# Three PSUM banks in turn, DVE work in half-chunk order, and the low part of x1 on GpSimd

## The chip, the cores and the metric

The kernel runs on one core of one Trainium2 chip. The metric is device time in microseconds (us), the median of the runs shown. Engines are named as in the profile: PE (TensorE), DVE (VectorE), ACT (ScalarE), POOL (GpSimd), SP (the queue that issues the DMAs). Each engine works through its own list of instructions in order, and semaphores order the engines against each other.

## The reference

```python
# layer 0, x: (4, 256, 64, 64)
k = conv(x, w1, 7x7, dilation 2, padding 6) + b1        # 256 -> 128 channels
k = conv(k, w2, 1x1) + b2                               # 128 -> 49 channels
attn = softmax(k, axis=1)                               # 49 weights at each pixel
x1 = einsum('bkchw,bkhw->bchw', shifts(x, 7x7, dilation 2), attn)
# layer 1: a bottleneck with batch norms over (0, 2, 3)
h = relu(bn(conv(x1, v1, 1x1)));  h = relu(bn(conv(h, v2, 3x3)));  h = bn(conv(h, v3, 1x1))
out = relu(h + x1)
```

## The kernel before

Because of the dilation by 2, each image splits into four independent images of 32x32 pixels ("images" from here on, 16 in all, `STEPS`). w1 and w2 are folded into one set of filters of 50 columns. Every fp32 operand of a product is split into a high part (rounded to fp32r) and a low part (the rest), and a product takes three matmuls (`mm3`). So each operand passes through an ACT copy (`..._hi`) and a subtraction (`..._lo`), on DVE or POOL.

**Preparation** (0 to 84 us). PE computes 14 groups of folded filters (L805, 14 matmuls in the profile for each) into the two banks `psX` in turn, ACT copies them (`wf`, `w_hi`), DVE forms sums of them (`filters`, L1036) and some low parts, POOL the other low parts (`filter_lo`). Between them DVE and POOL prepare the first signals of the convolution.

**The main loop** runs over 20 halves (`half(q)` of each engine), two for each pair of images. A Winograd-like convolution of a pair is 14 chunks (`ORDER`: points TWO, ONE, MINUS, HALF1, MHALF, ZERO, INF, for two channel blocks); an even half has the first 7, an odd half the last 7. Each chunk needs a signal: a sum of columns of `xbuf` (`whole`, L1063 on DVE or L546 on POOL), its high part (`sig_hi`, ACT) and its low part (`sig_lo`, POOL L551), in a ring of five. For point TWO DVE also rewrites the input buffer (`ab_of`: L1083 and L1089), and POOL then rewrites it once more (`c_of`, L558, 2304 columns in one instruction). `combine` (DVE, L1128 to L1147) forms the logits of ten output columns from the banks 0 to 2 of the points. In the next even half the softmax follows (`softmax_top`, `exponentials`, `softmax_end`), and its weights go out to DRAM and come back as bands (`scatter`, `load_raw`).

Three halves behind the convolution the same loop works on an image: PE transposes 8 band tiles (`band_T`, L848, all through the bank `psB`) and 4 pieces of x (`x_T`, L858, through `psXT`). ACT and DVE split them; ten `unit`s (L782 to L784) multiply them into `psX`, five for each half of the image's rows. `x_out` then copies `psX` to `x1_hi` and `x1` (ACT) and forms `x1_lo` (DVE, reading `psX`); `proj` (L888, through `psU`) multiplies x1 with v1; `yhalf` (ACT) and `y_out` (DVE, L1203 and L1205) finish it. "image" is the one at work, "tail" the one before it, whose second row half is finished in this half. PE walks through 15 parts in a half (two for each chunk), the others through 7 steps c.

After the loop come the batch norms, the 3x3 and the last 1x1 convolution (835 to 1031 us), which the change does not touch.

Of the kernel before, what the change touches and what calls it, by code (L numbers as in the profile page):

```python
# [9 lines left out]
ALU = mybir.AluOpType  # L10
# [104 lines left out]
(C_ONE, C_BIAS, C_SUM, C_DIFF, C_TWO), C_HALF, C_MHALF, C_ZERO, C_INF, COMBOS = range(5), 8, 12, 16, 17, 18  # L115


def build(nc, x, w1, b1, w2, b2, v1, g1, c1, v2, g2, c2, v3, g3, c3, out):
# [6 lines left out]
    with top:  # L125
# [9 lines left out]
        psXT, psB, psU = ps[:, 5, :], ps[:, 6, :], ps[:, 7, :]  # L135

# [17 lines left out]
        bias = sb(l0r, "bias", [P, KP])  # L154
# [77 lines left out]
        norm_done, probs_done = sem("norm_done"), sem("probs_done")  # L232
# [77 lines left out]
        def wait_slot(eng, g, t):  # L310

            if t >= 4:
                eng.wait_ge(unit_done, len(UNITS) * g + last_unit(t - 4) + 1)
            elif g:
                eng.wait_ge(unit_done, len(UNITS) * (g - 1) + last_unit(t + 4) + 1)

# [30 lines left out]
        def _(sp):  # L347
# [99 lines left out]
            def half(q):  # L447
                conv, first, image, tail, coming, soft = schedule(q)
                if tail is not None:
                    store_x1(tail, 1)  # L450
                if soft is not None:
                    spill(soft, 0)
# [64 lines left out]
        def _(pool):  # L517
            for t in (ident[:, :], gavg[:, :], up[:, :, :], dn[:, :, :], w2T[:, KK:KP], b2row[:, KK:KP]):
                pool.memset(t, 0.0).then_inc(consts, 1)
            for t in (ones[:, :], inside[:, :, :]):  # L520
                pool.memset(t, 1.0).then_inc(consts, 1)
            for c0, c1 in ((0, 2 * PAD), (2 * PAD + W, XC)):
                pool.memset(xbuf[:, :, 0:SH * XC].rearrange("p i (r c) -> p i r c", c=XC)[:, :, :, c0:c1], 0.0).then_inc(consts, 1)
            pool.memset(xbuf[:, :, SH * XC:XLEN], 0.0).then_inc(consts, 1)
            pool.wait_ge(consts, 11)
# [51 lines left out]

            def slot(k):

                if 0 <= k + RING - 1 < NCHUNK:  # L580
                    signal(k + RING - 1)
                if 0 <= k + RING - 2 < NCHUNK:
                    sig_lo(k + RING - 2)
                for i in range(2 * PAIRS):
                    if k == chunk_at(i // 2, TWO, i % 2) - RING + 3:
# [3 lines left out]

            for i in range(5):  # L590
                filter_lo(i)
            for k in range(1 - RING, 0):
                slot(k)
# [22 lines left out]
        def _(act):  # L616
# [6 lines left out]
            act.wait_ge(consts, 11)  # L623
# [12 lines left out]
            for i in range(CB * K):  # L636
                cb, v = divmod(i, K)
                act.wait_ge(weff_done, i + 1)
                if v in DIRECT:
                    copy(w_hi[:, cb, DIRECT[v], :], psX[i % 2][:, 0:NF]).then_inc(whi_done, 1)  # L640
                if cb:
                    act.wait_ge(wmade, MADE[3] if v <= 3 else MADE[6])
                copy(wf[:, v, :], psX[i % 2][:, 0:NF]).then_inc(wf_done, 1)
# [3 lines left out]
                if (cb, v) == (0, 5):  # L647
                    for k in range(RING - 2):
                        sig_hi(k)
# [19 lines left out]
            def xT(g, pt):  # L669
                act.wait_ge(xt_done, 4 * g + pt + 1)  # L670
                wait_slot(act, g, 2 * pt + 1)
                copy(xT_hi[:, 2 * pt % 4:2 * pt % 4 + 2, :], psXT.rearrange("p (t c) -> p t c", c=C)).then_inc(xT_hi_done, 1)

            def bandhi(g, t):
# [3 lines left out]
                copy(by_fours(band_hi[:, t % 4, band_rows(t), :]), window_of(psB[:, lo:hi])).then_inc(band_hi_done, 1)  # L678

            def yhalf(g, h):  # L680
# [3 lines left out]
                copy(y1[:, h, :], psU[MID1:P, :]).then_inc(yhalf_done, 1)  # L684
# [4 lines left out]

            def half(q):  # L690
                conv, first, image, tail, coming, soft = schedule(q)
                for c in range(SLOTS):
                    if image is not None:
                        if c in (0, 1, 2):
                            bandhi(image, c)
                    if c == 0 and tail is not None:
                        x_out(tail, 1)
                    if c == 0 and image is not None:
                        xT(image, 0)
                    if c == 2 and image is not None:  # L700
                        xT(image, 1)
                    if c == 3 and image is not None:
                        bandhi(image, 3)
                    if conv is not None and first + c + RING - 2 < NCHUNK:
                        sig_hi(first + c + RING - 2)
                    if c == 1 and tail is not None:
# [648 lines left out]
```

## Time and profile before

| what | value |
|---|---|
| median of 3 runs | 1032.48 us (1031.37 to 1032.67) |
| profiled execution, its own time | 1033.16 us |
| its span | 1031.4 us |
| mean granted TensorE clock | 0.940 of full speed |

The span runs from the first to the last instruction of the profiled execution; 1.8 us lie around it. Rows of a timeline give the start, the duration, the engine, the line, the operation with its tiles, and in brackets how long the engine sat idle before and what ended that.

### The profile page before, as it was taken

Reading aid. Unit: us, or ns where it says so; the run is one execution under the profiler, and the core shown is the slowest. Engines: PE = TensorE matmul, PEld = TensorE weight load, DVE = VectorE, ACT = ScalarE, POOL = GpSimd, SP = SyncE. Lnnn points to the kernel's source line nnn. Section 1 sums busy time; section 2 is a strip of 40 time slices with the busy share of each in tenths; the row PEclk is TensorE's granted clock in tenths of the full one; section 3 lists DMA queues with packets and bytes.
Section 4 is the critical chain, followed back from the end, with each engine's and each line's share of the span. In section 5 each row is a group of like instructions: output and inputs, shape, how many; then the busy total and the mean of one; then the engine's idle time right before and its main releaser. Section 6 shows DMA issues by size and latency. Waiting matters only on the chain.

```text
span 1031.4 us, 13805 instructions
## 1 busy us (share of the span) xinstructions
PE 870.8 (84%) x5084; PEld 815.1 (79%) x5084; DVE 670.4 (65%) x913; ACT 378.2 (37%) x647; POOL 321.5 (31%) x257
## 2 busy tenths in 40 slices
PE   5548969898998998999899899899667649969992
PEld 5548969898998998999899799899656537758882
DVE  1765677567778678676667767855544455139994
ACT  1222211243333433344344243333333466133267
POOL 2536455263255245227224524422200000004000
PEclk9999989999999999999899999999867869989997
DMA  9600224966775794885577576464687977000099
GB/s 287 211 0 1 42 53 104 204 176 149 166 194 133 172 202 114 207 178 163 156 173 180 146 174 151 124 188 109 177 206 194 209 269 296 1 1 1 26 388 401
DMA packets 261851, 163.11 MB, mean 158 GB/s; under 512 B 203817, under 2 KB 244762, under 8 KB 259226
## 3 DMA queue, kind: packets, MB, share of 16 engines
q1 hardware_dynamic: 261786, 162.24, 58.7%
q8 instruction: 41, 0.67, 0.3%
q14 instruction: 24, 0.20, 0.1%
HBM read 103.41 MB, written 53.97 MB: 153 GB/s over the span
## 4 chain that ended last, share of the span: by engine, by line
PE 49%; DVE 26%; DMA 8%; issue 7%; ACT 5%; POOL 2%; SPq 2%; DVEq 0%; ACTq 0%; POOLq 0%
PE ps L782 13%; PE ps L783 13%; PE ps L784 13%; DVE logit L1156 4%; DVE logit L1147 4%; DVE whole L1063 3%; PE ps L848 3%; DVE xbuf L1083 3%; DMA dn<-logit 3%; PE ps L888 3%; PE ps L805 2%; ACT y L774 2%; PE ps L858 2%; DMA out<-y 2%; DVE wsum L1036 2%
## 5 line engine op out<-in xcount | busy, mean ns | idle before, releaser
L782 PE MATMUL ps<-w_hi,ring 128*128 128x350 f32 x832 | 282.5, 340 | 12.1 <-DVE logit L1147 11.4
L784 PE MATMUL ps<-w_hi,ring 128*128 128x350 f32 x832 | 273.9, 329 | 0.0
L783 PE MATMUL ps<-w_lo,ring 128*128 128x350 f32 x832 | 273.5, 329 | 0.0
L551 POOL TENSOR_TENSOR ring<-whole,ring 128x576 fp32r<-128x576 f32 x112 | 168.2, 1503 | 263.5 <-ACT ring L618 263.5
L782 PEld LDWEIGHTS ps<-w_hi,ring 128*128 128x128 f32 x832 | 162.2, 195 | 13.4 <-issue 12.8
L783 PEld LDWEIGHTS ps<-w_lo,ring 128*128 128x128 f32 x832 | 161.8, 194 | 0.5
L784 PEld LDWEIGHTS ps<-w_hi,ring 128*128 128x128 f32 x832 | 160.9, 193 | 0.0
L618 ACT ACTIVATE ring<-whole 128x576 fp32r<-128x576 f32 x112 | 86.4, 775 | 142.3 <-DVE whole L1063 100.2
L618 ACT ACTIVATE band_hi<-ps 128x320 fp32r<-128x320 f32 (+1 forms) x128 | 53.6, 419 | 190.9 <-PE ps L848 190.7
L782 PE MATMUL ps<-band_hi,xT_hi 128*128 128x224 f32 (+2 forms) x320 | 99.2, 310 | 17.0 <-DVE x_lo L1000 10.0
L1000 DVE TENSOR_TENSOR band_lo<-ps,band_hi 128x320 fp32r<-128x320 f32 (+1 forms) x128 | 58.8, 459 | 72.5 <-ACT band_hi L618 72.4
L848 PE MATMUL ps<-ident,raw 128*128 128x128 f32 x352 | 64.8, 290 | 46.3 <-DVE band_lo L1000 42.5
L782 PE MATMUL ps<-h_hi,v_hi 128*128 128x512 f32 x224 | 90.9, 406 | 12.3 <-DVE h_lo L1000 12.3
L784 PE MATMUL ps<-band_hi,xT_lo 128*128 128x224 f32 (+2 forms) x320 | 95.2, 298 | 0.0
L783 PE MATMUL ps<-band_lo,xT_hi 128*128 128x224 f32 (+2 forms) x320 | 95.1, 297 | 0.0
L783 PE MATMUL ps<-h_lo,v_hi 128*128 128x512 f32 x224 | 90.4, 404 | 0.0
L784 PE MATMUL ps<-h_hi,v_lo 128*128 128x512 f32 x224 | 90.0, 402 | 0.0
L848 PEld LDWEIGHTS ps<-ident,raw 128*128 128x128 f32 x352 | 43.9, 148 | 56.5 <-issue 51.1
L1063 DVE SCALAR_TENSOR_TENSOR whole<-xbuf 128x576 f32<-128x576 f32 x80 | 74.5, 934 | 15.0 <-POOL ring L551 15.0
L782 PEld LDWEIGHTS ps<-band_hi,xT_hi 128*128 128x128 f32 x320 | 63.7, 199 | 20.6 <-DVE x_lo L1000 10.7
L612 POOL TENSOR_TENSOR h_lo<-y,h_hi 128x1024 fp32r<-128x1024 f32 x6 | 14.2, 2414 | 190.8 <-ACT h_hi L618 190.8
L1000 DVE TENSOR_TENSOR xT_lo<-ps,xT_hi 128x512 fp32r<-128x512 f32 x64 | 43.8, 685 | 42.3 <-ACT xT_hi L618 42.3
(127 smaller groups left out, 1435.2 us busy)
## 6 DMA issues: line engine op xcount, KB each, us to landing
xq<-in_x SPq DMA_DIRECT2D x128, 256.0 KB, 4.0
raw<-bands SPq DMA_DIRECT2D x32, 768.0 KB, 5.5
xbuf<-in_x SPq DMA_DIRECT2D x16, 1024.0 KB, 8.5
x_dram<-x SPq DMA_DIRECT2D x32, 512.0 KB, 2.8
x1in<-x_dram SPq DMA_DIRECT2D x8, 2048.0 KB, 17.0
out<-y SPq DMA_DIRECT2D x16, 1024.0 KB, 4.5
bands<-wide SPq DMA_DIRECT2D x32, 398.0 KB, 5.5
w1raw<-in_L_conv_w SPq DMA_DIRECT2D x2, 3136.0 KB, 12.6
```

Source lines behind the costliest of these rows:

```text
L551: pool.tensor_tensor(split(k, 1), positions(whole[:, k % TBUFS, :], 0, 2), split(k, 0).bitcast(F32), ALU.subtract).then_inc(sig_lo_done, 1)
L618: return act.activation(dst, src, ACT.Copy)
L782: pe.matmul(dst, l_hi, r_hi_, start=first, stop=False, **kw)
L783: pe.matmul(dst, l_hi, r_lo_, start=False, stop=False, **kw)
L784: return pe.matmul(dst, l_lo, r_hi_, start=False, stop=last, **kw)
L848: mm = pe.transpose(psB[:, i * P:(i + 1) * P], src, ident[:, :])
L888: mm = pe.matmul(psU, v1pack[:, cb, :], r[:, cb, :], start=(cb == 0 and j == 0), stop=(cb == CB - 1 and j == 1))
L1000: return dve.tensor_tensor(dst, a, b, ALU.subtract)
L1063: dve.scalar_tensor_tensor(out=dst, in0=a, scalar=factor, in1=b, op0=ALU.mult, op1=ALU.add).then_inc(done, 1)
L1083: dve.scalar_tensor_tensor(out=flat[:, 0:n], in0=flat[:, 0:n], scalar=-2.0, in1=flat[:, 2:n + 2], op0=ALU.mult, op1=ALU.add).then_inc(a_do ...
L1147: dve.scalar_tensor_tensor(out=dst, in0=m, scalar=factor, in1=src, op0=ALU.mult, op1=ALU.add).then_inc(comb_done, 1)
L1156: dve.scalar_tensor_tensor(out=part, in0=t[:, :, :], scalar=edge[:, i:i + 1], in1=part, op0=ALU.mult, op1=ALU.add).then_inc(add_done, 1)
```

## The change

Eight edits, all in the preparation and the main loop:

1. **Banks.** The filter groups use four banks (`psW`) instead of two. In the loop `band_T`, `x_T` and `proj` take the banks 5, 6 and 7 in one fixed rotation (`turns`): each waits for whoever used its bank three turns ago.
2. **Low part of x1.** `x_lo` on POOL reads `x1` and `x1_hi` from SBUF; `psX` is free as soon as ACT has copied it. In the three last halves, with no convolution, DVE does it.
3. **Order.** DVE and ACT go through 14 half-chunk parts. `proj(tail, 1)` moves from part 3 to 5 on PE, `proj(image, 0)` from part 13 to 14; `y_out(image, 0)` to the next half, and `y_out(tail, 1)` behind `softmax_end`.
4. **Combine.** 15 operations instead of 18 for a pair: the bias is added in the first one; ACT forms the product of HALF1 (`half_product`); the odd half has two operations on PSUM and four on SBUF alone, all behind the last MHALF chunk, where there were four behind HALF1 and four behind MHALF.
5. **c_of** in four pieces of 576 columns, each waiting for the one before.
6. **Softmax end**: one large product and a small one (112 columns) instead of two large ones.
7. **First signals** are made by DVE and POOL right after the first filter group.
8. **SP** spills logits ahead of `store_x1(tail, 1)`.

```diff
+        psW = [ps[:, 3, :], ps[:, 4, :], ps[:, 7, :], ps[:, 6, :]]
...
+            for kind, of, i in (("band", image, 0), ("x", image, 0), ("band", image, 1), ("band", image, 2),
+                                ("proj", tail, 1), ("x", image, 1), ("band", image, 3), ("band", image, 4),
+                                ("x", image, 2), ("band", image, 5), ("band", image, 6), ("x", image, 3),
+                                ("band", image, 7), ("proj", image, 0)):
+                if of is not None:
+                    turns.append((kind, of, i))
...
+        def take_bank(eng, kind, g, i):
+            n = turn_of[kind, g, i]
+            if n >= 3:
+                before, gb, ib = turns[n - 3]
+                if before == "band":
+                    eng.wait_ge(band_lo_done, NT * gb + ib + 1)
+                elif before == "x":
+                    eng.wait_ge(xT_lo_done, 4 * gb + ib + 1)
+                else:
+                    eng.wait_ge(y1_done, 2 * gb + ib + 1)
...
             def c_of(i):
                 pool.wait_ge(b_done, i + 1)
-                n = 2 * (SH * XC // 2)
-                pool.tensor_tensor(xflat(i)[:, 0:n], xflat(i)[:, 4:n + 4], xflat(i)[:, 0:n], ALU.subtract).then_inc(c_done, 1)
+                n = SH * XC // 4
+                for j in range(4):
+                    if j:
+                        pool.wait_ge(c_done, 4 * i + j)
+                    a, b = (xflat(i)[:, o + n * j:o + n * (j + 1)] for o in (0, 4))
+                    pool.tensor_tensor(a, b, a, ALU.subtract).then_inc(c_done, 1)
...
             def slot(k):
-                if 0 <= k + RING - 1 < NCHUNK:
+                q, c = divmod(k, SLOTS)
+                conv, first, image, tail, coming, soft = schedule(q)
+                if c == 1 and tail is not None:
+                    x_lo(tail, 1)
+                if c == 6 and image is not None:
+                    x_lo(image, 0)
+                if k + RING - 1 < NCHUNK:
                     signal(k + RING - 1)
...
                     if k == chunk_at(i // 2, TWO, i % 2) - RING + 3:
                         c_of(i)
```

ACT, `half`:

```diff
+                        if part == 10:
+                            bandhi(image, 6)
+                        if part == 11:
+                            x_out(image, 0)
...
+                    if part % 2 and conv is not None and first + part // 2 + RING - 2 < NCHUNK:
+                        sig_hi(first + part // 2 + RING - 2)
```

DVE, `half`:

```diff
+                        todo = ({10: (C_ONE,), 12: range(C_SUM, C_EVEN)} if q % 2 == 0 else
+                                {6: range(C_EVEN, C_ZERO), 12: (C_ZERO,)})
...
+                    if part == 7 and soft is not None:
+                        softmax_end(soft)
+                    if part == 7 and tail is not None:
                         y_out(tail, 1)
...
+                    if part % 2 and conv is not None:
+                        signal_slot(first + part // 2)
```

**POOL at the end of an odd half with an image.** The names: `whole<-pairs` is a signal, `ring<-whole,ring` a `sig_lo`, `xbuf<-xbuf` is `c_of`, `x_lo` the new low part of x1. Before:

```order
L546 TENSOR_TENSOR whole<-pairs 128x576 [waits sig_lo_done,b_done]
L551 TENSOR_TENSOR ring<-whole,ring 128x576 [waits sig_hi_done]
L546 TENSOR_TENSOR whole<-pairs 128x576 [waits sig_lo_done,b_done]
L551 TENSOR_TENSOR ring<-whole,ring 128x576 [waits sig_hi_done]
L558 TENSOR_TENSOR xbuf<-xbuf 128x2304 [waits b_done]
L551 TENSOR_TENSOR ring<-whole,ring 128x576 [waits sig_hi_done]
```

And now:

```order
L581 TENSOR_TENSOR ring<-whole,ring 128x576 [waits sig_hi_done]
L576 TENSOR_TENSOR whole<-pairs 128x576 [waits sig_lo_done,b_done]
L581 TENSOR_TENSOR ring<-whole,ring 128x576 [waits sig_hi_done]
L592 TENSOR_TENSOR xbuf<-xbuf 128x576 [waits b_done]
L592 TENSOR_TENSOR xbuf<-xbuf 128x576 [waits c_done] x3
L615 TENSOR_TENSOR x_lo<-x,x_hi 128x512 [waits x1_done] x2
```

The two `x_lo` stand behind the four pieces of `c_of`, and these behind a `sig_lo` that waits for ACT.

**DVE in an odd half, from the combine behind MHALF to the input rewrite.** `logit`, `mo` and `me` belong to combine, `whole`, `xbuf` and `pairs` to the signal of the next point TWO. Before:

```order
L1147 SCALAR_TENSOR_TENSOR logit<-ps,logit 128x500 [waits comb_done,chunk_done] x4
L1000 TENSOR_TENSOR band_lo<-ps,band_hi 128x320 [waits unit_done,band_hi_done] x2
L1063 SCALAR_TENSOR_TENSOR whole<-xbuf 128x576 [waits pads_done,x_loaded2,sig_lo_done]
L1063 SCALAR_TENSOR_TENSOR whole<-xbuf,whole 128x576 [waits sig_step]
L1083 SCALAR_TENSOR_TENSOR xbuf<-xbuf 128x2308 [waits sig_dve]
L1089 SCALAR_TENSOR_TENSOR pairs<-xbuf 128x1152 [waits sig_pool,a_done]
```

And now:

```order
L1209 SCALAR_TENSOR_TENSOR mo<-ps,me 128x500 [waits chunk_done,half_done,comb_done]
L1209 SCALAR_TENSOR_TENSOR me<-ps,me 128x500 [waits chunk_done,comb_done]
L1209 SCALAR_TENSOR_TENSOR logit<-mo,logit 128x500 [waits comb_done]
L1209 SCALAR_TENSOR_TENSOR logit<-me,logit 128x500 [waits comb_done]
...
L1066 TENSOR_TENSOR xT_lo<-ps,xT_hi 128x512 [waits unit_done,xT_hi_done]
L1066 TENSOR_TENSOR band_lo<-ps,band_hi 128x320 [waits unit_done,band_hi_done]
L1268 TENSOR_TENSOR y<-ps,y 64x512 [waits yhalf_done]
L1270 BN_STATS stats<-y 64x6 [waits y1_done]
L1130 SCALAR_TENSOR_TENSOR whole<-xbuf 128x576 [waits pads_done,x_loaded2,sig_lo_done]
```

Six operations (the two on `logit` come twice) now stand where four stood, and one `xT_lo` and `y_out(tail, 1)` have come in ahead of the signal.

**PE at the fifth band tile (t = 4).** `ident,raw` is `band_T`, `w_hi,ring` the convolution, `band_hi,xT_hi` a unit. Before:

```order
L784 MATMUL ps<-w_hi,ring 128x350
L848 MATMUL ps<-ident,raw 128x128 [waits band_lo_done,raw_loaded1,raw_loaded0]
L848 MATMUL ps<-ident,raw 128x128 x2
L782 MATMUL ps<-band_hi,xT_hi 128x320 [waits xT_lo_done,band_lo_done]
L783 MATMUL ps<-band_lo,xT_hi 128x320
```

And now:

```order
L842 MATMUL ps<-w_hi,ring 128x350
L909 MATMUL ps<-ident,raw 128x128 [waits y1_done,raw_loaded1,raw_loaded0]
L909 MATMUL ps<-ident,raw 128x128 x2
L840 MATMUL ps<-w_hi,ring 128x350
L841 MATMUL ps<-w_lo,ring 128x350
```

The tile waited for the `band_lo` before it; it now waits for `y_out(tail, 1)`, whose bank it takes, and its unit comes half a chunk later.

## Rows read from the trace of the kernel before

**Rows 1.** The page: span and busy time of the engines.

```profile
span 1031.4 us, 13805 instructions
...
PE 870.8 (84%) x5084; PEld 815.1 (79%) x5084; DVE 670.4 (65%) x913; ACT 378.2 (37%) x647; POOL 321.5 (31%) x257
```

**Rows 2.** Windows: preparation, loop with images, last halves (stretch, length, busy).

```profile
0.00:84.00 84.00, 45.71 (x204) 44.70 (x204) 44.80 (x63) 18.59 (x40) 33.97 (x41) 1.00 0.52 153
...
191.00:721.00 530.00, 496.48 (x3269) 483.94 (x3267) 377.67 (x508) 199.41 (x362) 210.49 (x156) 0.98 0.67 164
721.00:835.00 114.00, 74.36 (x419) 66.28 (x417) 51.85 (x90) 42.22 (x89) 5.33 (x12) 0.78 0.76 190
```

**Rows 3.** Timeline of PE in the preparation: filter groups.

```profile
12.91 18.66 PE L805 MATMUL ps<-w2T,w1raw 128*128 128x50 f32 x84 [2.48 <-DMA w1raw<-in_L_conv_w]
...
64.66 12.48 PE L805 MATMUL ps<-w2T,w1raw 128*128 128x50 f32 x56 [14.78 <-DVE w_lo L1000]
```

**Rows 4.** Timeline of PE: an odd half (268.85 on), the even half behind it.

```profile
268.85 0.38 PE L848 MATMUL ps<-ident,raw 128*128 128x128 f32 x2
287.64 0.52 PE L848 MATMUL ps<-ident,raw 128*128 128x128 f32 x3 [0.48 <-DVE band_lo L1000]
295.36 0.28 PE L782 MATMUL ps<-band_hi,xT_hi 128*128 128x96 f32 x1 [0.97 <-DVE xT_lo L1000]
302.53 0.48 PE L888 MATMUL ps<-x_hi,v1pack 128*128 128x512 f32 x1
307.61 0.38 PE L848 MATMUL ps<-ident,raw 128*128 128x128 f32 x2
326.43 0.52 PE L848 MATMUL ps<-ident,raw 128*128 128x128 f32 x3 [3.53 <-DVE band_lo L1000]
353.85 0.38 PE L848 MATMUL ps<-ident,raw 128*128 128x128 f32 x2
```

**Rows 5.** Timeline of DVE in the same odd half.

```profile
284.07 3.03 DVE L1147 SCALAR_TENSOR_TENSOR logit<-ps,logit 128x500 f32<-128x500 f32 x4
289.07 0.76 DVE L1063 SCALAR_TENSOR_TENSOR whole<-xbuf 128x576 f32<-128x576 f32 x1
290.66 2.56 DVE L1083 SCALAR_TENSOR_TENSOR xbuf<-xbuf 128x2308 f32<-128x2308 f32 x1
293.25 1.36 DVE L1089 SCALAR_TENSOR_TENSOR pairs<-xbuf 128x1152 f32<-128x1152 f32 x1
300.46 0.68 DVE L1147 SCALAR_TENSOR_TENSOR logit<-ps,logit 128x500 f32<-128x500 f32 x1 [0.62 <-PE ps L784]
305.09 0.69 DVE L1205 BATCH_NORM_STATS2 stats<-y 64x6 f32<-64x512 f32 x1
```

**Rows 6.** Timeline of ACT there: the copies of x1, and a sig_hi.

```profile
297.90 1.11 ACT L618 ACTIVATE x<-ps 128x512 f32<-128x512 f32 x2
298.85 0.82 ACT L618 ACTIVATE ring<-whole 128x576 fp32r<-128x576 f32 x1
```

**Rows 7.** Timeline of POOL: sig_lo, c_of in both halves.

```profile
283.49 1.93 POOL L551 TENSOR_TENSOR ring<-whole,ring 128x576 fp32r<-128x576 f32 x1 [6.63 <-ACT ring L618]
...
298.46 1.43 POOL L551 TENSOR_TENSOR ring<-whole,ring 128x576 fp32r<-128x576 f32 x1
299.86 4.03 POOL L558 TENSOR_TENSOR xbuf<-xbuf 128x2304 f32<-128x2304 f32 x1
...
316.45 4.58 POOL L558 TENSOR_TENSOR xbuf<-xbuf 128x2304 f32<-128x2304 f32 x1
```

**Rows 8.** Timeline of DVE in the even half: the top of the softmax.

```profile
315.95 1.19 DVE L1156 SCALAR_TENSOR_TENSOR logit<-up,edge,logit 128x600 f32<-128x600 f32 x1 [1.65 <-DMA dn<-logit]
317.18 4.50 DVE L1156 SCALAR_TENSOR_TENSOR logit<-dn,edge,logit 128x600 f32<-128x600 f32 x1
```

**Rows 9.** Groups by line: POOL subtractions with an fp32r result.

```profile
L612 POOL TENSOR_TENSOR h_lo<-y,h_hi 128x1024 fp32r<-128x1024 f32 x6 | 14.2, 2414 | 190.8 <-ACT h_hi L618 190.8
```

**Rows 10.** Timeline of PE at the start of the second pair.

```profile
153.53 0.63 PE L782 MATMUL ps<-w_hi,ring 128*128 128x350 f32 x1 [9.59 <-DVE logit L1147]
```

More of the change, by code:

```diff
@@ L588, in slot @@
                         pads(i)
+            signal(1)
+            sig_lo(0)
+            signal(2)
+            sig_lo(1)
+            sig_lo(2)
             for i in range(5):
                 filter_lo(i)
-            for k in range(1 - RING, 0):
-                slot(k)
+            c_of(0)
             for i in range(5, CB * len(WHOLES)):
@@ L688, in exponentials, with half_product @@
                 act.activation(probs[:, :, :, :], probs[:, :, :, :], ACT.Exp).then_inc(exp_done, 1)
+            def half_product(s):
+                act.wait_ge(chunk_done, chunk_at(s, HALF1, CB - 1) + 1)
+                act.wait_ge(comb_done, comb(s, C_EVEN - 1))
+                act.activation(me[:, :], ps[:, BANKS[HALF1], 0:BANK], ACT.Copy, scale=16 / 9).then_inc(half_done, 1)
             def half(q):
                 conv, first, image, tail, coming, soft = schedule(q)
-                for c in range(SLOTS):
-                    if image is not None:
[L694 to L706, printed above, removed]
@@ new lines, in half @@
+                for part in range(2 * SLOTS):
+                    if part == 0 and tail is not None:
+                        x_out(tail, 1)
+                    if part == 4 and q % 2 == 1 and conv is not None:
+                        half_product(conv)
+                    if image is not None:
+                        if part in (0, 2, 4):
+                            bandhi(image, part // 2)
+                        if part in (1, 5, 8):
+                            xT(image, part // 3)
+                        if part == 6:
+                            bandhi(image, 3)
+                        if part == 7:
+                            bandhi(image, 4)
+                        if part == 9:
+                            bandhi(image, 5)
+                        if part == 10:
+                            bandhi(image, 6)
+                        if part == 11:
+                            x_out(image, 0)
+                    if part == 6 and tail is not None:
@@ L1240, in half @@
-                    if c == 6 and image is not None:
-                        xT(image, 3)
-                        bandlo(image, 7)
-                        y_out(image, 0)
-                    if conv is not None:
-                        signal_slot(first + c)
+                    if part == 2 and conv is None and tail is not None:
+                        x_lo(tail, 1)
+                    if part == 4 and soft is not None:
+                        softmax_top(soft)
+                    if image is not None:
+                        if part in (1, 3, 5):
+                            bandlo(image, part // 2)
+                        if part in (2, 6, 9):
+                            xT(image, (2, 6, 9).index(part))
+                        if part in (7, 8):
+                            bandlo(image, part - 4)
+                        if part in (10, 11):
+                            bandlo(image, part - 5)
```

238 lines of the change are left out of this document (118 added, 120 removed).

## The prediction

> **What bounds the kernel now.** I read the page first [rows 1]: PE is busy for 870.8 of 1031.4 us, DVE for 670.4, POOL for 321.5. So the question is where PE waits. The windows [rows 2] split it: in the preparation PE is busy for 45.7 of 84.0 us, in the 530 us of the loop with images for 496.5, in the last halves for 74.4 of 114. The timeline of PE shows what ends the waits. In the preparation it is DVE: one filter group waits 14.78 us for a `w_lo` that stands behind filter sums and the input rewrite [rows 3]. In the loop a pair takes 85.0 us (268.85 to 353.85), an odd half 38.8 and an even half 46.2 [rows 4]. The odd half has two small waits (0.48 and 0.97); the even half has one of 3.53 us at a band tile. That tile waits for a `band_lo` behind the top of the softmax, whose second operation took 4.50 us because POOL was in `c_of` from 316.45 on for 4.58 us [rows 8, 7].
>
> That row is worth a closer look. The first softmax operation came at 315.95, took 1.19 us and ended at 317.14; `c_of` was issued at 316.45 and ended at 321.03; the second operation then ended at 321.68. So whichever of the two engines waits gets the next turn, for a whole instruction. POOL waits likewise: a `sig_lo` of 1.43 us took 1.93 beside a `whole` on DVE [rows 7]. DVE's combine of 0.68 us at 300.46, which reads one operand from PSUM, lost nothing beside the `c_of` of 299.86 [rows 5, 7]. So two SBUF operands are what matters. The Trainium skill (SBUF — State Buffer, "SBUF: two separate sides") calls the shared port pair an exclusive lock, held for the whole instruction, and names DVE operations with two SBUF inputs; by this rule, the trace agrees. By a rule of shared bandwidth the third term below would be near zero.
>
> **The change, part by part.** The sum is made against the profiled execution's 1033.2 us, 0.7 above the median.
>
> *Preparation: -20 us.* A filter group takes 3.1 us (four in 12.48) and the first starts at 12.91 [rows 3]. With four banks the first eleven run on to about 47. DVE's work is still in series: sums of one block, their second part, the rewrite for the second input (1.5, 2.56 and 1.36 us, as in the loop [rows 5]); but the first rewrite now fills time in which DVE waited for filter copies. I put the `w_lo` that releases the twelfth group at 54.5. Three groups follow, and the convolution starts near 64 in place of 84.0. Bounds: -12, if DVE and the earlier `c_of` block each other more, and -24.
>
> *Combine and the fifth band tile, odd half: +3.6 us.* Before, four operations in 3.03 us (0.77 each) began at 284.07, and the tile was released at 287.64 [rows 5, 4]. Now six operations stand there (+1.55), then an `xT_lo`, `band_lo`, and `y_out`, 0.7 us each by the nearest row (0.69 at 305.09), and PE waits for the last: about 290.4 for work ready at 287.1. Behind it DVE's signal starts at 291 instead of 289.07, and a `sig_lo` of 1.4 us, which ACT now releases just then, gets in between its two operations. The rewrite (2.56 and 1.36) ends 3.3 us later, the `xT_lo` behind it too, and the unit that started at 295.36 now starts at 299.0. That PE's waits take this form is why the rotation gains little here: the bank that the tile takes is that of the slowest user.
>
> *proj(image, 0) in an odd half with c_of: +9.4 us.* Follow the queues from that unit, at 299.0. ACT copies x1 (four copies, two in 1.11 us [rows 6]), done at 302.5, and only then makes `sig_hi` (0.8), which stood ahead of the copies before. POOL's `sig_lo` ends at 304.7. Now comes `c_of`. A piece costs about 1.15 us: 4.03 / 4 = 1.0 is the lower bound [rows 7], the fixed part of an instruction adds to it. Then the two `x_lo`: half of 2.41 us for 1024 columns, 1.2 to 1.27 each [rows 9]. PE meanwhile needs 7.2 us from the unit to proj as before (295.36 to 302.53), and 1.8 more, since 12 of the 34 matmuls of the next 5.08 us now stand ahead of proj [rows 4]: it is there at 307.9. POOL alone would be done at 312.2. But DVE's two signals, 2.56 and 1.36 (5.4 us in all) are released at 305.2 by the last ZERO chunk, and turn by turn with the pieces they go in ahead of `x_lo`: it ends at 317.2, and proj waits 9.4 us. Bounds: 4.3 (no DVE operation gets in) and 10.5.
>
> *Clock: +1.6 us in each of these.* After the idle 9.59 us the first matmul took 0.63 us, twice a usual one [rows 10], and the last halves, which are full of waits, have a granted clock of 0.78, the loop 0.98 [rows 2]. I take 1.6 us, as if some 3 us of work behind the wait ran at the lower of the clock's two levels (1.2 in place of 2.4 GHz). Bounds 0 and 2.
>
> *Even half: -1.5 us, six times.* The 3.53 us go, and about 1.5 behind them (the loop's granted clock of 0.98 is 1.7 us in a pair of 85 [rows 2]), since the softmax now starts well before PE needs it. In their place the fifth tile waits for `y_out(tail, 1)` behind `band_hi`, `yhalf`, the exponentials and `softmax_end`: 2.4 us, some lock turns, and some clock. Bounds: -3 and +1.
>
> *The rest.* The half with q = 15 has no `c_of`: +3, the tile alone. The first two pairs: 0 (a shorter combine, but the pieces and the rewrite again share turns; -3 to +2). The last halves: -7 (the spill no longer waits for `store_x1`, units wait for ACT's copies alone); they idle 40 us [rows 2], bounds -15 and 0. DVE loses 64 `x_lo`, 24 combine operations and 8 large products: nothing, except where said, as DVE is idle a third of the time [rows 1].
>
> Sum: six odd halves 6 x 14.6 = 87.6, less 2.6 for the first, which has no tail (85); even halves -9; preparation -20; q = 15 +3; last halves -7; +52. So 1033.2 + 52 = 1085, less 0.7 for the median: **1084 us**. Its own range is 1066 to 1098.
>
> **The rivals.**
> - *POOL keeps its turn*: `c_of` and `x_lo` run through, and DVE follows. proj waits 4.3 instead of 9.4 us: 6 x 5.1 = 31 less, 1054 us. Against it stands the 1.19 us operation of [rows 8], which got in between two POOL instructions. Chance 0.16.
> - *The combine does not delay the unit*: the tile's wait is absorbed as the second one of 0.97 us partly is. 6 x 3.6 = 22 less, 1062 us. Chance 0.12.
> - *Faster*: the low part is ready in time, because POOL gets to `c_of` earlier than I think (it would have to start 9 us earlier relative to proj, or the queue order lets ACT release `sig_lo` before the copies). Then six halves cost 3.6 at most, or nothing, and the preparation and the last halves remain: 1033 - 20 - 7 - 9 + 3 + (0 to 20), 1000 to 1020 us. It decides at a cost of (20 + 9 + 7 - 3) / 6 = 5.5 us for an odd half; I have 14.6, and 9.5 at the lower bound of the lock. For it: DVE loses 60 us of work, and the waits of [rows 4] for `band_lo` do go. Chance 0.22.
> - *The preparation does not gain*: the twelfth group is released as late as before. Then 1104. Chance 0.04.
>
> The Trainium skill (GPSIMD Engine Reference, "Performance versus the Vector engine") has GpSimd about two times slower than DVE for such a subtraction. That alone would cost nothing here, as POOL is idle two thirds of the time; it is the place in POOL's queue that costs.
>
> **How the numbers follow.** My forecast has 0.44; rivals 0.16, 0.12, 0.22, 0.04; 0.02 for no change. A difference under 0.2% (2 us) is about what a measurement cannot tell from none. Range 1008 to 1096: it leaves out the lower half of the faster case and the preparation rival. Faster 0.22, same 0.02, slower 0.76.
>
> **What would show it.** Right: convolution starts near 64 us; in each odd half with `c_of` PE waits 8 to 10 us at proj for `x_lo` on POOL, and 2 to 4 us at the fifth band tile for `y`; DVE's `whole`, `xbuf` and `pairs` alternate with four POOL pieces; a pair takes about 98 us. Wrong: proj without a wait, or a pair under 88 us; then the order of release on POOL is not what I followed.

## The result: slower, 1082.3 us

The changed kernel takes 1082.3 us (median of 4 runs, 1082.0 to 1083.2) beside 1032.5 us for the kernel before on the same chip (4 runs): 1.0486 times the time, 95% interval 1.0472 to 1.0500. The profiled execution took 1083.2 us. Its page answers to [rows 1]:

```profile
span 1081.4 us, 13756 instructions
PE 893.0 (83%) x5084; PEld 837.8 (77%) x5084; DVE 634.3 (59%) x839; ACT 375.3 (35%) x655; POOL 438.8 (41%) x356
```

DVE is busy 36 us less, POOL 117 us more, and the span is 50 us longer: the engine that was relieved was not the one that set the time. What PE waited for (engine, line, what it waited for, us in total, times, longest), two rows of the view of waits:

```profile
PE ps L947 <- POOL x_lo L615: 46.0, 6, 8.2
PE ps L909 <- DVE y L1268: 43.8, 16, 4.9
```

The same waits in the timeline of PE: two filter groups (compare [rows 3]), then the fifth band tile of an even and of an odd half and `proj(image, 0)` of that odd half (compare [rows 4]).

```profile
38.36 9.42 PE L865 MATMUL ps<-w2T,w1raw 128*128 128x50 f32 x42 [0.68 <-DVE w_lo L1066]
55.62 0.65 PE L865 MATMUL ps<-w2T,w1raw 128*128 128x50 f32 x2 [7.85 <-DVE w_lo L1066]
64.82 0.64 PE L840 MATMUL ps<-w_hi,ring 128*128 128x350 f32 x1
235.98 0.52 PE L909 MATMUL ps<-ident,raw 128*128 128x128 f32 x3 [2.47 <-DVE y L1268]
281.32 0.52 PE L909 MATMUL ps<-ident,raw 128*128 128x128 f32 x3 [2.98 <-DVE y L1268]
306.75 0.79 PE L947 MATMUL ps<-x_hi,v1pack 128*128 128x512 f32 x1 [8.18 <-POOL x_lo L615]
```

The convolution starts at 64.8 us instead of 84.0. The fifth tile waits for `y`, and `proj`, which had no wait before, waits 8.18 us. Why it does is read from POOL and DVE in the same odd half (POOL's rows first, then DVE's, then the last two copies of x1 on ACT; compare [rows 5, 6, 7]):

```profile
293.96 1.42 POOL L581 TENSOR_TENSOR ring<-whole,ring 128x576 fp32r<-128x576 f32 x1 [1.63 <-ACT ring L668]
295.33 7.81 POOL L592 TENSOR_TENSOR xbuf<-xbuf 128x576 f32<-128x576 f32 x4
303.11 3.59 POOL L615 TENSOR_TENSOR x_lo<-x,x_hi 128x512 fp32r<-128x512 f32 x2
...
295.83 1.27 DVE L1130 SCALAR_TENSOR_TENSOR whole<-xbuf 128x576 f32<-128x576 f32 x1
297.13 1.59 DVE L1130 SCALAR_TENSOR_TENSOR whole<-xbuf,whole 128x576 f32<-128x576 f32 x1
298.75 3.39 DVE L1150 SCALAR_TENSOR_TENSOR xbuf<-xbuf 128x2308 f32<-128x2308 f32 x1
302.18 2.18 DVE L1156 SCALAR_TENSOR_TENSOR pairs<-xbuf 128x1152 f32<-128x1152 f32 x1
...
292.12 1.10 ACT L668 ACTIVATE x<-ps 128x512 f32<-128x512 f32 x2
```

x1 was copied at 293.2 (last ACT copy), PE was ready for proj at 298.58, `x_lo` ended at 306.70. Four pieces of `c_of` took 7.81 us of POOL, and the view of these four by tile shows why (minimum, median and maximum of a piece, in ns):

```profile
L592 POOL TENSOR_TENSOR xbuf<-xbuf x4: 1148/1542/3347, 295.3 to 299.8; 128x576 f32<-128x576 f32 x4
```

An undisturbed piece is 1.15 us. The last one came at 299.8, while DVE was in `xbuf`, and took 3.35 us, so it waited 2.2 us. The `xbuf` operation had waited in its turn for the piece ahead: it took 3.39 us, where 2.56 are usual [rows 5]. The Trainium skill (SBUF — State Buffer, "SBUF: two separate sides") has the shared port pair as an exclusive lock rather than shared bandwidth; the row agrees.

Behind the wait the granted clock is at its lower level (windows: stretch, length, busy time and count of PE, PEld, DVE, ACT, POOL, then the granted clock):

```profile
306.70:308.90 2.20, 2.15 (x6) 1.76 (x7) 0.00 (x0) 0.04 (x1) 2.06 (x3) 0.50 0.47 130
308.90:313.00 4.10, 4.10 (x21) 4.10 (x20) 1.37 (x2) 0.56 (x2) 0.46 (x1) 0.56 0.03 8
313.00:320.00 7.00, 7.00 (x48) 6.99 (x47) 2.74 (x4) 4.70 (x9) 3.04 (x3) 1.00 0.61 149
```

0.50 is 1.2 of 2.4 GHz. The four matmuls of proj took 2.08 us and the 18 of the units behind it 4.34; in the even half ahead, without a wait, they took 1.09 and 2.60. So 8.2 us of wait cost another 2.7 us.

Where the 50 us arise is read from the starts of `proj(image, 0)` in both timelines, a mark that every half has:

| stretch (us) | before | after | difference | forecast |
|---|---|---|---|---|
| start to proj of the first odd half with an image | 217.5 | 210.2 | -7.3 | -8 (-20 preparation, 0 first pairs, +12 that half) |
| from there five pairs, to proj of q = 13 | 425.8 | 479.9 | +54.1 | +65.5 |
| one more pair, to q = 15 (no c_of) | 84.5 | 86.7 | +2.2 | +1.5 |
| to proj of the last image's second half | 101.6 | 102.4 | +0.8 | -7 |
| the rest | 202.0 | 202.2 | +0.2 | 0 |

### The profile page after: what moved, and what is told of

It is laid out like the page before. It is cut to its first block, busy times and chain, and to the rows that moved or that the text cites. A ratio compares the mean times of both kernels' runs of the same rounds, so it can differ in the third digit from the quotient of the medians.

```text
span 1081.4 us, 13756 instructions
## 1 busy us (share of the span) xinstructions
PE 893.0 (83%) x5084; PEld 837.8 (77%) x5084; DVE 634.3 (59%) x839; ACT 375.3 (35%) x655; POOL 438.8 (41%) x356
## 4 chain that ended last, share of the span: by engine, by line
PE 54%; DVE 21%; POOL 9%; ACT 6%; DMA 4%; issue 4%; SPq 1%; ACTq 0%; DVEq 0%; POOLq 0%
PE ps L840 14%; PE ps L841 14%; PE ps L842 14%; POOL xbuf L592 4%; DVE stats L1377 4%; PE ps L947 4%; PE ps L909 3%; DVE x1in L1389 3%; PE ps L918 2%; POOL x_lo L615 2%; PE ps L865 2%; DVE logit L1209 2%; POOL ring L581 2%; ACT y L832 2%; DVE whole L1130 1%
## 5 line engine op out<-in xcount | busy, mean ns | idle before, releaser
L840 PE MATMUL ps<-w_hi,ring 128*128 128x350 f32 x832 | 288.3, 346 | 11.0 <-DVE logit L1209 10.0
L581 POOL TENSOR_TENSOR ring<-whole,ring 128x576 fp32r<-128x576 f32 x112 | 171.9, 1537 | 288.9 <-ACT ring L668 288.9
L842 PE MATMUL ps<-w_hi,ring 128*128 128x350 f32 x832 | 275.4, 331 | 0.0
L840 PEld LDWEIGHTS ps<-w_hi,ring 128*128 128x128 f32 x832 | 164.2, 197 | 11.8 <-issue 10.6
L841 PEld LDWEIGHTS ps<-w_lo,ring 128*128 128x128 f32 x832 | 163.6, 197 | 0.0
L842 PEld LDWEIGHTS ps<-w_hi,ring 128*128 128x128 f32 x832 | 162.7, 196 | 0.0
L909 PE MATMUL ps<-ident,raw 128*128 128x128 f32 x352 | 66.5, 296 | 52.0 <-DVE y L1268 43.8
L840 PE MATMUL ps<-band_hi,xT_hi 128*128 128x224 f32 (+2 forms) x320 | 102.5, 320 | 7.4 <-DVE xT_lo L1066 4.7
L592 POOL TENSOR_TENSOR xbuf<-xbuf 128x576 f32<-128x576 f32 x64 | 101.6, 1588 | 3.8
L841 PE MATMUL ps<-band_lo,xT_hi 128*128 128x224 f32 (+2 forms) x320 | 100.3, 313 | 0.0
L842 PE MATMUL ps<-band_hi,xT_lo 128*128 128x224 f32 (+2 forms) x320 | 99.8, 312 | 0.0
L1130 DVE SCALAR_TENSOR_TENSOR whole<-xbuf 128x576 f32<-128x576 f32 x80 | 81.1, 1018 | 20.4 <-POOL ring L581 20.3
L668 ACT ACTIVATE xT_hi<-ps 128x512 fp32r<-128x512 f32 x64 | 38.5, 602 | 150.7 <-PE ps L918 106.6
## 6 DMA issues: line engine op xcount, KB each, us to landing
x1in<-x_dram SPq DMA_DIRECT2D x8, 2048.0 KB, 17.1
```

The source lines that it names most:

```text
L581: pool.tensor_tensor(split(k, 1), positions(whole[:, k % TBUFS, :], 0, 2), split(k, 0).bitcast(F32), ALU.subtract).then_inc(sig_lo_done, 1)
L592: pool.tensor_tensor(a, b, a, ALU.subtract).then_inc(c_done, 1)
L668: return act.activation(dst, src, ACT.Copy)
L840: pe.matmul(dst, l_hi, r_hi_, start=first, stop=False, **kw)
L841: pe.matmul(dst, l_hi, r_lo_, start=False, stop=False, **kw)
L842: return pe.matmul(dst, l_lo, r_hi_, start=False, stop=last, **kw)
```

## Experiments

The kernel before was measured again on the chip of each run below, and took 1031.3 to 1032.7 us there.

**Theory.** In an odd half three results come out of their queues within a few us of each other: `y_out` behind the combine (DVE), `x_lo` behind `c_of` (POOL), and the low parts `xT_lo` and `band_lo` behind the rewrite (`xbuf`, `pairs`, DVE). The change made all three late; the one that PE meets first shows in the trace and hides the others. **Rival.** The position of `x_lo` on POOL alone is the loss, and putting it right gives it back. A second rival is that the two engines share bandwidth, so that the number of pieces and the order don't matter.

### before_prep: the preparation alone

The kernel before, with four banks for the filter groups, the first signals behind the first filter copy, and POOL's order there; its loop is untouched.

```diff
-                if (cb, v) == (0, 4):
+                if (cb, v) == (0, 0):
                     for k in range(1 - RING, -1):
                         signal_slot(k)
...
-                    mm = pe.matmul(psX[i % 2][:, p * KP:(p + 1) * KP], ...
+                    mm = pe.matmul(psW[i % 4][:, p * KP:(p + 1) * KP], ...
```

> The kernel before with only the preparation of the change: filter groups over four banks, first signals made among the filter sums, their order on POOL; loop unchanged. Theory (the preparation gives 19 to 20 us and the loop alone loses 69): convolution starts near 65 us instead of 84.0, total 1032.5 - 19 = 1011 to 1016 us. Rival (the earlier start is lost in the first pairs, which wait for something else): 1020 to 1033 us.

Measured: 1014.3 us, within the theory's range; ratio 0.9821 (0.9802 to 0.9840). The last block of filter groups on PE starts at 56.3 and ends at 65.7:

```profile
56.30 9.42 PE L813 MATMUL ps<-w2T,w1raw 128*128 128x50 f32 x42 [8.56 <-DVE w_lo L1008]
```

So the preparation is worth 18.4 us and keeps it to the end. The rest of the change costs 1082.3 - 1014.3 = 68 us.

### xlo_first and xlo_dve: x_lo out of c_of's shadow

`xlo_first` moves the two `x_lo` of POOL ahead of `c_of`:

```diff
-                if c == 6 and image is not None:
-                    x_lo(image, 0)
                 if k + RING - 1 < NCHUNK:
                     signal(k + RING - 1)
                 if k + RING - 2 < NCHUNK:
                     sig_lo(k + RING - 2)
+                if c == 5 and image is not None:
+                    x_lo(image, 0)
```

> The changed kernel with one move: on POOL the two x_lo of the odd half stand ahead of c_of instead of behind it. Theory (place in the queue): x1 is copied at 293.2, the sig_lo ahead ends at 295.3, so the two x_lo (3.1 us in the even half) end near 298.5 and proj, which PE reaches at 298.6, no longer waits 8.2 us. But xT_lo and band_lo 7 stand behind DVE's rewrite until 305.2, and PE would want them about 302.1: a new wait of about 3 us there. Net 5 to 6.5 us for each of six odd halves: 1043 to 1052 us. Rival 1 (the shared turns set it, wherever x_lo stands): the signal on DVE gets in, x_lo ends past 301, proj still waits 2 to 3: 1058 to 1065. Rival 2 (DVE's rewrite is the real chain, the wait for x_lo only hides it): PE waits as long one unit later, above 1072.

`xlo_dve` gives `x_lo` back to DVE, at its old places (`x_lo(tail, 1)` in part 1, `x_lo(image, 0)` in part 11).

```diff
+                        if part == 11:
+                            x_lo(image, 0)
```

> The changed kernel with x_lo on DVE, where it stood before, all else as in the change. Theory (proj's wait is only the first of two that end nearly together): proj waits for nothing or under 1 us, the unit behind it waits 4 to 5 us for xT_lo behind the rewrite, as with x_lo first on POOL: 1068 to 1078 us. Rival (moving x_lo to POOL is the whole loss of the odd half): 6 x 9 = 54 less, 1025 to 1035 us.

Measured: 1074.7 us (1073.5 to 1075.2) for `xlo_first`, 23 us above its theory's range, and 1071.1 us (1070.4 to 1075.3) for `xlo_dve`, as expected. The wait at proj is gone in both, and the next unit but one stands instead (xlo_first, then xlo_dve):

```profile
304.53 0.60 PE L840 MATMUL ps<-band_hi,xT_hi 128*128 128x320 f32 x1 [4.90 <-DVE xT_lo L1066]
```
```profile
307.11 0.58 PE L836 MATMUL ps<-band_hi,xT_hi 128*128 128x320 f32 x1 [4.77 <-DVE xT_lo L1062]
```

46 us of waits were removed and 7.6 or 11.2 us gained. That holds for POOL and for DVE alike, so the engine that does `x_lo` is not the point. I had expected 30 to 39 us from `xlo_first`, with a wait of 3 us at the unit. PE comes to it earlier than I reckoned: 2.05 us after it began proj at 297.58, not 3.5; and `xT_lo` ends at 304.39.

### cof_whole: c_of in one piece

```diff
-                n = SH * XC // 4
-                for j in range(4): ...
+                n = SH * XC
+                a, b = (xflat(i)[:, o:o + n] for o in (0, 4))
+                pool.tensor_tensor(a, b, a, ALU.subtract).then_inc(c_done, 4)
```

> The changed kernel with c_of in one instruction again instead of four. Theory (turns by whole instructions): only one DVE operation gets in ahead of each POOL instruction; c_of 4.0 us from 295.3, then whole, x_lo, whole, x_lo, done at about 303.3 instead of 306.7; the rewrite follows later, so a unit behind proj waits 1 to 2 us. Net 2 to 3 us for each of six odd halves: 1064 to 1070 us. Rival (the engines share the port's bandwidth, or the number of pieces does not matter): 1080 to 1084.

Measured: 1090.4 us (1087.7 to 1095.1), 8 us more where both expectations had it no slower. proj waits 3.1 us in the same pair instead of 8.18, as expected, but the unit behind it waits 2.5 for `xT_lo`, the clock stays low for longer (0.50 and 0.70 in the stretches 306:310 and 310:320), and from the fifth tile of the even half to that of the next odd one it takes 1.6 us more (45.4 against 43.8). In the same odd half a unit ahead of proj waits 1.53 us, for an `xT_lo` behind the rewrite. One wait of 8.2 us became three of 1.5, 3.1 and 2.5, and a full pair became a little longer, not shorter (96.4 us against 95.8). The pair that ends with q = 15 has no `c_of` at its end, so it has the loss without the gain: 92.9 against 86.7 us.

### y_early: y_out(tail, 1) ahead of the combine and of softmax_end

```diff
+                    if part == 6 and tail is not None and conv is not None and q % 2 == 1:
+                        if image is not None:
+                            xT(image, 1)
+                            bandlo(image, 3)
+                        y_out(tail, 1)
...
+                    if part == 7 and tail is not None and not early:
+                        y_out(tail, 1)
                     if part == 7 and soft is not None:
                         softmax_end(soft)
-                    if part == 7 and tail is not None:
-                        y_out(tail, 1)
```

> The changed kernel with y_out(tail, 1) earlier on DVE: in odd halves ahead of the six combine operations (with xT_lo 1 and band_lo 3 ahead of it), in even halves ahead of the end of the softmax. Theory (the fifth tile waits for the bank that proj used, and only for that): the waits of 3.0 and 2.5 us vanish and with them slow work of about 1 us behind each; the chain from the unit to proj shifts as a whole, so proj still waits about 8 us. Net 3 to 4.5 us in each of some 12 halves, 36 to 50 us: 1032 to 1046 us. Rival (the wait only hides the next one: signals and rewrite on DVE, released by the pads and chunks, set the unit and proj): tile waits vanish, but the unit or proj waits longer, 1065 to 1080.

Measured: 1063.9 us (1062.9 to 1065.4), 18.4 less, 18 above the theory's range and just under the rival's. The tile waits are gone in both halves. In the even half that is a gain; in the odd half the unit behind waits 5 us, again for an `xT_lo`, and then proj as before:

```profile
285.17 0.42 PE L840 MATMUL ps<-band_hi,xT_hi 128*128 128x96 f32 x1 [5.04 <-DVE xT_lo L1066]
```
```profile
303.45 0.79 PE L947 MATMUL ps<-x_hi,v1pack 128*128 128x512 f32 x1 [6.57 <-POOL x_lo L615]
```

### xlo_lows and best: the low parts ahead of the rewrite

`xlo_lows` is `xlo_first` with the low parts moved: `xT_lo` 2 between `xbuf` and `pairs`, `xT_lo` 3 and `band_lo` 7 ahead of `xbuf`. `best` has `y_early` as well.

```diff
                 flat = xflat(i)
+                for f in ahead:
+                    f()
                 dve.scalar_tensor_tensor(out=flat[:, 0:n], ...
+                for f in between:
+                    f()
                 dve.wait_ge(a_done, i + 1)
...
                         signal_slot(first + part // 2,
+                                    (lambda: xT(image, 3), lambda: bandlo(image, 7)) if split_up and part == 13 else (),
+                                    (lambda: xT(image, 2),) if split_up and part == 7 else ())
```

> x_lo ahead of c_of and the low parts ahead of the rewrite, y_out where the change put it. Theory: the 4.9 us for xT_lo behind proj go, which x_lo first alone brought to light (7.6 us gained of 46 waited); the fifth tile still waits 3.0 and 2.5 us. Six odd halves gain 7 to 9 us each against the changed kernel: 1028 to 1040 us. Rival (POOL and DVE are full there, the wait only moves to a third place): 1060 to 1075.

> The changed kernel with three changes of order together: x_lo ahead of c_of on POOL; y_out(tail, 1) early; and the low parts that stood behind DVE's rewrite of the input ahead of its parts (xT_lo 2 between xbuf and pairs, xT_lo 3 and band_lo 7 ahead of xbuf). Theory (in an odd half three queues end within a few us of each other: y_out, x_lo behind c_of, the lows behind the rewrite; each removed alone shows the next): all three together leave a pair at 82 to 84 us in place of 96.1, 6 x 13 = 78 less, 997 to 1010 us, faster than before. Rival 1 (a fourth thing is next, a chunk that waits for its signal behind the rewrite): 1015 to 1035. Rival 2 (the low parts do not matter, POOL is simply full in the odd half): 1050 and more.

Measured: xlo_lows 1049.0 us (1047.1 to 1052.3), best 1010.5 us (1008.7 to 1011.9), ratio 0.9792 (0.9774 to 0.9810) to the kernel before. `xlo_lows` missed its range by 9 us: proj still waits 2.3 us behind the waiting tile. `best` came out half a us above its range, and its pair takes 85.5 us, not 82 to 84. Yet the pattern is the theory's:

| out of the way | us | less than the change |
|---|---|---|
| x_lo | 1074.7 | 7.6 |
| y_out | 1063.9 | 18.4 |
| x_lo, low parts | 1049.0 | 33.3 |
| x_lo, low parts, y_out | 1010.5 | 71.8 |

`y_out` is worth 18.4 us in the changed kernel and 38.5 us once the others are out of the way. In the five pairs from q = 3 on alone it is 10.3 and 25.2 us. The low parts were not moved alone, so what they are worth by themselves is not measured.

The repair undoes the loss of the loop and does no more. From the profiled executions, with the marks at the first band tile of a half (us):

| stretch | before | before_prep | change | best |
|---|---|---|---|---|
| start to q = 3, the first half with an image | 183.2 | 164.0 | 163.6 | 163.7 |
| five pairs from there | 426.4 | 425.7 | 479.8 | 426.9 |
| the rest | 421.8 | 422.8 | 438.0 | 419.6 |

What `best` gains on the kernel before is the preparation, and some 2 us at the end. (`best3`, further down, brings the five pairs to 423.2.)

### best_whole: one piece of c_of again

> The same three changes of order, and c_of in one instruction. In the changed kernel one piece instead of four cost 8 us. Theory A (one piece holds DVE's low parts and rewrite back, and these are waited for): with the low parts ahead it costs at most 3 us. Theory B (one piece costs DVE time as such, in the softmax as well): it still costs 6 to 10 us against the run with four pieces.

Measured: 1030.9 us (10 runs, 1028.3 to 1034.5), 20.4 more than `best`. So theory A fell, and the 6 to 10 us of B were too few. With less other waiting the one piece costs more, not less. DVE and POOL at that place with one piece:

```profile
293.74 4.48 DVE L1127 SCALAR_TENSOR_TENSOR whole<-xbuf,whole 128x576 f32<-128x576 f32 x1
298.25 0.69 DVE L1063 TENSOR_TENSOR xT_lo<-ps,xT_hi 128x512 fp32r<-128x512 f32 x1
```
```profile
293.05 4.56 POOL L589 TENSOR_TENSOR xbuf<-xbuf 128x2304 f32<-128x2304 f32 x1
```

and with four:

```profile
289.28 1.60 DVE L1130 SCALAR_TENSOR_TENSOR whole<-xbuf,whole 128x576 f32<-128x576 f32 x1
290.91 0.69 DVE L1066 TENSOR_TENSOR xT_lo<-ps,xT_hi 128x512 fp32r<-128x512 f32 x1
```

The `whole` that PE's `xT_lo` stands behind is held for all of `c_of`, 4.5 us instead of 1.6, and PE waits for that `xT_lo` in each odd half, 1.9 to 2.8 us, here from 296.69 to 299.09. `c_of` itself took 4.56 us there and 4.03 undisturbed [rows 7], so the two engines don't share a bandwidth: one waits for nearly the whole instruction of the other. Short pieces are the better form in both orders, by 8.1 us in the changed kernel and by 20.4 us here.

### best2, best3, best4: the last wait of a pair

`best` has one wait of 4.83 us left in a pair, for a `band_lo` behind the rewrite:

```profile
278.28 0.45 PE L840 MATMUL ps<-band_hi,xT_hi 128*128 128x96 f32 x1 [4.83 <-DVE band_lo L1066]
```

Three versions try to remove it. `best2` puts `band_lo` 4 ahead of DVE's signals, `xT_lo` 2 ahead of the rewrite, and the last four combine operations behind it:

```diff
+                                {6: range(C_EVEN, C_HALF), 8: range(C_HALF, C_ZERO), 12: (C_ZERO,)} if split_up and tail is not None else
                                 {6: range(C_EVEN, C_ZERO), 12: (C_ZERO,)})
...
+                        if part == 7 and split_up:
+                            if not early:
+                                bandlo(image, 3)
+                            bandlo(image, 4)
```

> The version with three changes of order, and a fourth: in the odd half band_lo 4 goes ahead of DVE's signals, xT_lo 2 ahead of the rewrite, and the last four combine operations, which only add into logit, behind it. Theory (the one wait of 4.8 us left in a pair is for the band_lo that still stands behind the rewrite, and some 2 us of slow clock come with it): 6 x 5.5 to 7 us less than 1010.5, so 968 to 980 us. Rival (the combine or the chunks of the next pair are late in their turn): 985 to 1010.

Measured: 1006.0 us (999.4 to 1006.5). PE now waits for `raw`, from DMA, in the next half. The rows of SP's queue say why, `best` first:

```profile
271.91 4.33 SPq L436 DMA_DIRECT2D up<-logit  x1
...
278.51 1.02 SPq L460 DMA_DIRECT2D raw<-bands  x1
```
```profile
275.70 0.91 SPq L436 DMA_DIRECT2D up<-logit  x1
...
278.89 0.96 SPq L460 DMA_DIRECT2D raw<-bands  x1
```
```profile
286.24 0.44 PE L909 MATMUL ps<-ident,raw 128*128 128x128 f32 x2 [2.65 <-DMA raw<-bands]
```

The spill of `logit` (`up`, `dn`) waits for the combine, and the loads of `xq` and `raw` wait behind it in SP's order. In `best` the load goes out at 278.51 and PE starts the next half at 293.56, 15.1 us later. In `best2` PE is ready for that half at 283.59, 4.7 us after the load, which takes 7.4 us to land (median of the DMA view from 270 to 300). Counted from the fifth band tile of the half before, the load goes out after 11.8 us in `best` and after 17.8 in `best2`. `best3` therefore leaves the combine and puts only the low parts in front:

```diff
+                        if part == 7 and split_up:
+                            if not early:
+                                bandlo(image, 3)
+                            bandlo(image, 4)
+                            xT(image, 2)
```

> As the version with three changes of order (1010.5 us), but in the odd half band_lo 4 and xT_lo 2 stand ahead of DVE's two signals, behind all six combine operations, so that the spill of logit on SP is released as early as there. Theory (the 4.8 us wait is for band_lo behind the rewrite; the version that moved the combine made it up by a late spill, SP's queue, and a late load of raw): both waits go, a pair takes 79 to 82 us instead of 85.7, 970 to 986 us. Rival (a pair of 85.6 us in both versions is the period of something else, a loop over combine, spill, softmax and raw): 1000 to 1008 us, with a wait for DMA at the band tiles.

Measured: 1005.7 us (1004.4 to 1006.4), ratio 0.9737 (0.9723 to 0.9750), in the rival's range but without the wait that the rival named. In the pairs the wait for `band_lo` and the one for DMA are gone, and proj waits 4.37 us for `x_lo`, which stands on POOL behind two signals. `best4` puts `x_lo` ahead of them (`c == 5 - q % 2`):

> The run before with x_lo one step earlier again on POOL: in an odd half ahead of the two signals that wait for pairs (slot 4), in an even half ahead of sig_lo of slot 5. There x1 was copied at 275.6, POOL stood idle until 276.6, and x_lo ended at 284.7 behind two signals and two sig_lo, 4.4 us after PE wanted it. Theory (this wait, with the slow clock behind it, is the last one of a pair): 5.5 to 6.5 us in six odd halves, 966 to 975 us; a pair takes 78 to 80 us. Rival (POOL's two signals, now 2.5 us later, hold up a chunk, or the softmax comes next): 985 to 1000 us.

Measured: 1011.2 us (1009.0 to 1012.0), 5.5 more. Its only wait in a pair is 6.01 us, for the `xT_lo` behind DVE's `whole`, which is late since POOL's signals are. The remaining waits of best3 and best4 side by side:

```profile
284.76 0.80 PE L947 MATMUL ps<-x_hi,v1pack 128*128 128x512 f32 x1 [4.37 <-POOL x_lo L615]
```
```profile
290.85 0.61 PE L840 MATMUL ps<-band_hi,xT_hi 128*128 128x320 f32 x1 [6.01 <-DVE xT_lo L1066]
```

A pair (mean of four) takes 85.5, 85.6, 84.7 and 85.5 us in best, best2, best3 and best4, and 85.2 in the kernel before. All three forecasts of 966 to 986 us were wrong. Each order moves the wait to another result and leaves the pair as long; what sets this length stays open. One candidate is the series rewrite, POOL's signal, `sig_hi`, `sig_lo`, DVE's `whole` (in best3 DVE sits idle for 3.89 us before that `whole`, until a `sig_lo` of POOL); it was not tested, and a version with `xT_lo` 3 ahead of `whole`, or a third buffer for `whole`, was not run.

### xlo_behind: x_lo put back behind c_of, in best3

> The same, with x_lo behind c_of again on POOL, as the change has it: what this one position costs when no other wait lies beside it. Theory (x_lo first alone gained only 7.6 us since the unit behind proj waited for xT_lo at nearly the same time): put back alone it costs the whole term, proj waits 5 to 8 us in six odd halves and 1 to 2 us of slow clock come with it, 36 to 60 us more than the run beside it. Rival (with DVE's low parts ahead of the rewrite POOL gets through c_of sooner, and x_lo is nearly in time): 0 to 15 us more.

Measured: 1051.6 us (1050.7 to 1051.9), 46.0 more than `best3` on the same chip, within the theory's 36 to 60.

```profile
302.49 0.79 PE L947 MATMUL ps<-x_hi,v1pack 128*128 128x512 f32 x1 [12.83 <-POOL x_lo L615]
```

The wait goes from 4.37 to 12.83 us: 8.5 in each of five odd halves and 8.4 in the first, 51 us in the six. The same position that was worth 7.6 us in the changed kernel is worth 46 us where nothing waits beside it. This is the test that separates the theory from its rival.

## Why the prediction was right, point by point

1084 us was forecast and 1082.3 measured; the likeliest case, both waits and their places, was the one that came. That the total is within 2 us is luck in part: the five pairs cost 11.4 us less than the sum had, the last halves 7.8 more. Its terms:

- **Preparation, -20.** Right: the convolution starts 19.2 us earlier, the twelfth filter group at 55.6 (its release was put at 54.5), and alone it is worth 18.4 us (`before_prep`).
- **Combine and the fifth tile, +3.6.** Right: from the combine to the tile 6.0 us (forecast 6.3), a wait of 2.98 (3.3), and from the start of the half to the unit behind the tile 29.6 us against 26.5 before, so +3.1. The forecast had `xT_lo` behind the rewrite set that unit. In the trace `xT_lo` ended at 289.43 and PE came at 289.57, so there the two nearly met: the longer wait and the slow matmuls behind it already cost PE as much.
- **proj behind c_of, +9.4.** Right in kind, 1.2 too large. Counted from the unit: x1 copied after 3.6 us (forecast 3.5), `sig_lo` done after 5.8 (5.7), PE at proj after 9.0 (8.9), `x_lo` done after 17.1 (18.2). The turns were taken as described, and `pairs` went in beside `x_lo`.
- **Clock, +1.6 in an odd half.** Mis-sized: 2.7 us behind the 8.2 us wait alone, outside the bound of 2. The 1.5 us behind the 2.98 us wait (12 convolution matmuls in 3.71 instead of 2.17) lie inside the 3.1 above.
- **An odd half in all, +14.6.** 52.8 us (260.0 to 312.8) against 38.8, so +14.0, which is 3.1 + 8.2 + 2.7: proj and the tile were put 1.7 too high, the clock 1.1 too low.
- **Even half, -1.5.** Mis-sized: 43.3 us against 46.2, so -2.9 in this pair, at the bound of -3 (-1.4 in the first pair, -2.9 to -3.7 in the others). The wait of 2.46 us is the one forecast, but the 12 convolution matmuls behind it took 2.15 us here, the usual time, where 2.91 were taken in the first pair. The sum has 65.5 us for the five pairs, the trace 54.1: of the 11.4 between them 6.4 lie in the even halves, the rest in the odd ones.
- **q = 15, +3, and the first pairs, 0.** Right within 1 us.
- **Last halves, -7.** Wrong: +0.8. The waits that I counted on did go (three of 3.3 us for `x_lo` at a unit), but others came: for `y`, 4.28 and 1.28 us at a fifth tile and 4.87 at a second one, and 8.9 instead of 6.7 us for `x_lo` at the last proj. The term was made from what the diff removes, without following the queues of these halves as in the odd half.
- **DVE's work.** It lost 50 `x_lo`, not 64: 14 stay on DVE in the last halves. That changes nothing in the sum.
- **The rivals.** POOL does not keep its turn. "The preparation does not gain" and "the unit is not delayed" fell. "Faster" needed an odd half at 5.5 us or less; it was 14.0. The sum was right although one reading in it was incomplete: it put the loss at proj on the queue position alone. `xlo_first` shows that the low parts behind the rewrite would have cost nearly as much there by themselves; the forecast for that repair was 23 us too low at its upper end. One sentence of the working does not hold: that with shared bandwidth the term at proj would be near zero. Its own lower bound, with no DVE operation in between, is 4.3 us, since `x_lo` stands behind `c_of` by either rule.

## What to carry to other kernels

A wait in a trace, with the slow matmuls behind it (2.7 us behind one of 8.2), is at most what its removal gives; ask which result the same engine needs next, in which queue it stands, and when it leaves it. When several queues end nearly together, repairs have to be made together and measured together: 7.6 and 18.4 us for two of the repairs alone, 71.8 us for all three. An idle engine is no reason to give it work: what counts is what stands ahead of the work in its queue and who takes turns with it. And apply the part of a change that pays by itself: the preparation alone gives 1014.3 us; with the repaired loop on top, `best3`, it is 1005.7 us, 27.1 us under the kernel before on the same chip.

## Not expected of the hardware

- Splitting an instruction that holds the port shared by DVE and POOL made the other engine's work faster by more than it cost: 20.4 us for 16 `c_of`. POOL's time in `c_of` rose (107.0 us in all in `best`, 72.4 in `best_whole`), but the 96 `whole` of DVE took 99 us instead of 139.
- `sig_lo`, 1.4 us, can take its turn within the combine as well since the change: an operation `logit<-me,logit` of 0.68 us took 1.78 in `best3` at 266.85 beside a `sig_lo` of 1.47 us at 266.63, where [rows 5] had the combine read PSUM and lose nothing.
- `x_lo` of 512 columns took 1.27 us on POOL undisturbed (2.54 for two in `best`) and 0.685 us on DVE (mean in `xlo_dve`), 1.9 times. The Trainium skill (GPSIMD Engine Reference, "Performance versus the Vector engine") has about two; the rows agree.
